# First layer of a two-layer graph network: x loads ahead of the adjacency, three quarters of the mask as strips on GpSimd

## The reference, cut to what matters

```
h = relu(layernorm(x))
q, k, v = h @ W.T + b, in 4 heads of 64
scores = clip(q @ k.T / 8, -10, 10), and -10 where adj == 0
attn = softmax(scores) within each chunk of 256 keys
out = (sum over the 8 chunks of attn @ v) @ Wo.T + bo + h
x = x + layernorm(out) * gamma + beta
...                         # second layer: softmax over neighbours of leaky_relu(ei + ej)
```

## Time and profile before

| | |
|---|---|
| median of 3 runs | 4966.05 us (4965.57 to 4966.41) |
| profiled execution | 4965.84 us, span 4964.0 us |
| busy, share of the span | TensorE 4617.1 us (93%), VectorE 3681.5 (74%), ScalarE 2924.1 (59%), GpSimd 1947.7 (39%) |
| mean of one clip (L512), of one exponential (L421) | 1216 ns, 1056 ns |
| mean granted TensorE clock | 0.98 |
| TensorE busy in 25 to 50, 50 to 75, 75 to 100, 107 to 175 us | 13.00, 25.00, 9.56, 67.60 us |
| GpSimd busy in 0 to 25, 50 to 150 us | 15.76, 0.00 us |

### The profile page before, as it was taken

The page is one execution under the profiler, slowest core; times in us unless marked ns, Lnnn a source line. Parts: engine busy times, 40 slices in busy tenths (PEclk is TensorE's granted clock), DMA queues, the critical chain, the costliest instruction groups (busy, mean ns, idle before and its releaser), DMA issues. The chain is left out here.

```text
span 4964.0 us, 78134 instructions
## 1 busy us (share of the span) xinstructions
PE 4617.1 (93%) x31752; PEld 2705.9 (55%) x31752; DVE 3681.5 (74%) x5434; ACT 2924.1 (59%) x3373; POOL 1947.7 (39%) x1391
## 2 busy tenths in 40 slices
PE   5999999998999999999999899947999999999998
PEld 2334333333433433433333343327999999999998
DVE  4676677678577677667767857747889889898896
ACT  3553555455455355355445545518878888788785
POOL 1133222232232223223223323225657576666585
PEclk9999999999999999999999999968999999999999
DMA  5000000000100000000000000011112112111111
GB/s 186 1 18 9 26 9 18 26 9 9 34 9 9 19 16 18 9 26 14 13 26 9 13 14 9 9 35 49 50 47 77 30 68 76 34 65 54 47 56 44
DMA packets 126665, 160.50 MB, mean 32 GB/s; under 512 B 8545, under 2 KB 108897, under 8 KB 126305
## 3 DMA queue, kind: packets, MB, share of 16 engines
q1 hardware_dynamic: 126304, 155.49, 9.7%
HBM read 121.64 MB, written 33.83 MB: 31 GB/s over the span
## 5 line engine op out<-in xcount | busy, mean ns | idle before, releaser
L421 ACT ACTIVATE e_sb<-e_sb 128x1024 f32<-128x1024 f32 x1024 | 1080.4, 1056 | 1186.6 <-DVE e_sb L512 1171.4
L512 DVE SCALAR_TENSOR_TENSOR e_sb<-psS,mask 128x1024 f32<-128x1024 f32 x1024 | 1225.8, 1216 | 473.8 <-PE psS L628 460.1
L1229 PE MATMUL psA<-xy,ring_p 128*128 128x195 bf16 x8192 | 1399.4, 248 | 19.6 <-DVE red L1109 19.6
L1229 PE MATMUL psA<-xy,ring_s 128*128 128x195 bf16 x8192 | 1399.0, 248 | 0.0
L628 PE MATMUL psS<-qT,kT 64*128 64x512 f32 x4096 | 1089.7, 617 | 57.3 <-DVE e_sb L512 57.3
L1029 ACT ACTIVATE ring_s<-eiB,ejb 128x1024 int8<-128x1024 f32 x1024 | 1088.5, 1135 | 8.5 <-PE psA L1229 8.5
L641 PE MATMUL psN<-e_sb,v_sb 128*64 128x512 f32 x4096 | 1000.1, 609 | 0.0
L352 POOL TENSOR_TENSOR ctxT<-ctxT,num 128x512 f32<-128x512 f32 x384 | 486.3, 1275 | 1009.0 <-DVE num L492 1009.0
L1229 PEld LDWEIGHTS psA<-xy,ring_p 128*128 128x128 fp8e4 x8192 | 799.5, 98 | 24.9 <-DVE red L1109 22.5
L1229 PEld LDWEIGHTS psA<-xy,ring_s 128*128 128x128 fp8e4 x8192 | 798.7, 97 | 8.0 <-issue 0.3
L628 PEld LDWEIGHTS psS<-qT,kT 64*128 64x128 f32 x4096 | 460.2, 187 | 464.2 <-issue 234.7
(11 more groups left out here) (104 smaller groups left out, 4010.5 us busy)
## 6 DMA issues: line engine op xcount, KB each, us to landing
eiB<-ei_between SPq DMA_DIRECT2D x64, 512.0 KB, 4.2
xin<-x SPq DMA_DIRECT2D x32, 512.0 KB, 6.7
xr<-x SPq DMA_DIRECT2D x32, 512.0 KB, 3.8
x_between<-hy SPq DMA_DIRECT2D x32, 512.0 KB, 2.9
xin<-x_between SPq DMA_DIRECT2D x32, 512.0 KB, 5.6
xo<-x_between SPq DMA_DIRECT2D x32, 512.0 KB, 4.4
out<-o_sb SPq DMA_DIRECT2D x32, 512.0 KB, 5.2
e_sb<-adjT SPq DMA_DIRECT2D x4, 2048.0 KB, 9.6
```

The lines of the kernel that those rows point to most:

```text
L421: act.activation(e_sb[:, s % ES], e_sb[:, s % ES], ACT.Exp, scale=SCALE).then_inc(exp_done, 1)
L512: dve.scalar_tensor_tensor(out=e_sb[:, s % ES], in0=psS[:, s % 2], scalar=-CLIP_RAW, in1=mask[:, kb, cols][:, None, :].to_broadcast([P, 2, ...
L1229: ins = pe.matmul(psA[:, i % BANKS, br * PARTS * XW:(br + 1) * PARTS * XW], part[:, n % RING, k, tt * TW + j * P:tt * TW + (j + 1) * P], x ...
```

## The change

x tiles 2 and 3 are issued ahead of any adjacency. Only the adjacency of query tile 0 is still loaded in two halves and converted by VectorE and ScalarE, now at v = 15 (`MASK_AT`), and the steps begin when these two are done. The adjacency of query tiles 1 to 3 comes as 24 strips of 2 key blocks x 512 columns (0.5 MB), which lie by turns in xr and hy, two buffers that the first layer uses later for the residual. Each strip is issued when the one before the last has been converted. GpSimd converts all of them, after its constants and ahead of its first sum. VectorE waits for eight strips at the first step of each further tile of the first batch; the first load of a residual waits for all 24. The next batch's x is issued behind the last strip.

```diff
-MASK_AT = 5
+MASK_AT = 15
...
+        strip = [v.rearrange("p j f -> p (j f)").bitcast(I32).rearrange("p (k w) -> p k w", k=2) for v in (xr[:, :, :], hy[:, :, :])]
+        STRIPS = BLK // 2
+
+        def strip_at(m):
+
+            t, k = m // STRIPS + 1, m % STRIPS * 2
+            return slice(k, k + 2), slice(t * TW, (t + 1) * TW)
+
...
+            def load_strip(m):
+                if m >= 2:
+                    sp.wait_ge(strip_done, m - 1)
+                blocks, cols = strip_at(m)
+                sp.dma_start(strip[m % 2], adj_v[:, blocks, cols]).then_inc(strip_in[m % 2], 16)
...
             def load_residual(b, t):
+                if b == 0 and t == 0:
+                    sp.wait_ge(strip_done, (T - 1) * STRIPS)
                 sp.wait_ge(x1_out, b * (16 * T) + 16 * t + 16)
...
-            load_adjacency(0)
             load_x(0, 2)
             load_x(0, 3)
-            load_adjacency(1)
-            load_adjacency(2)
-            load_adjacency(3)
+            load_adjacency()
+            for m in range((T - 1) * STRIPS):
+                load_strip(m)
...
             pool.wait_ge(const_in, 16 * NCONST)
+            for m in range((T - 1) * STRIPS):
+                blocks, cols = strip_at(m)
+                pool.wait_ge(strip_in[m % 2], 16 * (m // 2 + 1))
+                pool.tensor_scalar(mask[:, blocks, cols], strip[m % 2], 2 * CLIP_RAW, -CLIP_RAW, ALU.mult, ALU.add)\
+                    .then_inc(strip_done, 1)
...
-            act.wait_ge(mask_done[0], T)
-            act.wait_ge(mask_done[1], T)
+            act.wait_ge(mask_done[0], 1)
+            act.wait_ge(mask_done[1], 1)
...
+                    if b == 0 and s % STEPS == 0 and s:
+                        dve.wait_ge(strip_done, s // STEPS * STRIPS)
                     dve.wait_ge(scores_done, b * BSTEPS + s + 1)
...
-            dve.wait_ge(mask_done[0], T)
-            dve.wait_ge(mask_done[1], T)
+            dve.wait_ge(mask_done[0], 1)
+            dve.wait_ge(mask_done[1], 1)
```

More of the change, by code:

```diff
@@ L157, in layer0 @@
         mask_done = [sem(f"mask_done{i}") for i in range(2)]
+        strip_in = [sem(f"strip_in{i}") for i in range(2)]
+        strip_done = sem("strip_done")
         ident_done = sem("ident_done")
@@ L246, in load_x, with load_adjacency @@
                 sp.dma_start(xin[:, t], tile_of(x_v, b, t)).then_inc(x_in[t], 16)
-            def load_adjacency(t):
+            def load_adjacency():
                 for k in range(2):
-                    if t >= 1:
-                        sp.wait_ge(mask_done[k], t)
-                    sp.dma_start(stage[k], adj_v[:, 8 * k:8 * k + 8, t * TW:(t + 1) * TW]).then_inc(adj_in[k], 16)
+                    sp.dma_start(stage[k], adj_v[:, 8 * k:8 * k + 8, 0:TW]).then_inc(adj_in[k], 16)
+            def load_strip(m):
[3 more added lines that the diff above has]
+                sp.dma_start(strip[m % 2], adj_v[:, blocks, cols]).then_inc(strip_in[m % 2], 16)
             def load_residual(b, t):
+                if b == 0 and t == 0:
+                    sp.wait_ge(strip_done, (T - 1) * STRIPS)
                 sp.wait_ge(x1_out, b * (16 * T) + 16 * t + 16)
@@ L435, in _ @@
                 prepare(0, v)
[L436 to L439, removed]
+                if v == MASK_AT:
+                    act.wait_ge(adj_in[1], 16)
+                    act.activation(mask[:, 8:16, 0:TW], stage[1], ACT.Copy,
                                    bias=-CLIP_RAW, scale=2 * CLIP_RAW).then_inc(mask_done[1], 1)
-            act.wait_ge(mask_done[0], T)
-            act.wait_ge(mask_done[1], T)
+            act.wait_ge(mask_done[0], 1)
+            act.wait_ge(mask_done[1], 1)
             for b in range(nb):
@@ L549, in _ @@
                 prepare(0, v)
[L550 to L553, removed]
+                if v == MASK_AT:
+                    dve.wait_ge(adj_in[0], 16)
+                    dve.tensor_scalar(mask[:, 0:8, 0:TW], stage[0], 2 * CLIP_RAW, -CLIP_RAW,
                                       ALU.mult, ALU.add).then_inc(mask_done[0], 1)
             dve.wait_ge(consts_done, 1)
-            dve.wait_ge(mask_done[0], T)
-            dve.wait_ge(mask_done[1], T)
+            dve.wait_ge(mask_done[0], 1)
+            dve.wait_ge(mask_done[1], 1)
             for b in range(nb):
```

## The result

The changed kernel takes 4937.47 us (median of 6 runs, 4936.16 to 4939.30), the kernel before on the same chip 4966.23. The ratio is 0.9943 with a 95% interval of 0.993 to 0.9956: 28.8 us less. The forecast was 4938.9. The profiled execution of the changed kernel was the slowest of its six, 4939.30 us with a span of 4937.4; against the profiled 4965.84 it is 26.5 us less, where the sum said 26.9.

A forecast was written before the change was run, and what follows sets the result against it. TensorE, busy 93% of the span, was taken as the bound, with time to win only in its start-up waits. 10.7 + 16.5 - 0.3 = 26.9 us off 4965.84 gave 4938.9 us, range 4934 to 4945.

The forecast's parts named there:

- Step 1: Start-up loads: x tile 2 ahead of the adjacency lands at 15.1, first projection at 26.3; net gain 10.7 us.
- rival (a): Start-up loads: the queue mixes x with the adjacency, so x comes no earlier; only 16.5 us gained, 4949.3; 6%.
- The rule on shared ports: SBUF access: two-SBUF-input VectorE instructions and GpSimd instructions take turns, each for its whole length; forecast charged 0.2 us instead.
- Rival (c): Statistics chains and mask conversion: VectorE and GpSimd take turns, leaving 19.2 us of gain, 4946.6; 6%.
- Step 2: First projection to first scores: stays 45.6 us, no gain; slow first matmuls worth some 1.8 us either way.
- Step 3: First clip no longer waits for masks 2 to 4: gain 16.5 us, less 0.3 for VectorE's conversion meeting strips.
- Step 4: GpSimd's 24 strips: 1.3 us conversion, 3.8 us load, 2.6 us spacing, done at 91, at worst 106; cost nothing.
- the cover: Ahead of GpSimd's first sum at 134: 28 us to spare for strips; beyond it each microsecond would count in full.
- Sum: Whole kernel: 10.7 + 16.5 - 0.3 = 26.9 us gained at the head of the chain; nothing later changes.

The follow-up runs named there:

- e1: The kernel before with only the loads reordered, x tiles 2 and 3 ahead of the adjacency, all masks converted as before: 4954.71 us.
- e2: The changed kernel with its strips, but x tiles 2 and 3 loaded behind the adjacency of query tile 0 again: 4950.39 us.
- e8: The changed kernel with VectorE's half of the first mask converted four times, each behind a wait for the one before: 4948.24 us.
- e6: The changed kernel with 64 small identity matmuls on TensorE between the first transposes and the first projection: 4936.37 us.
- e9: e5 with ScalarE normalising x tile 3 behind the first k copies, plus 36 small identity matmuls ahead of TensorE's first transposes: 4923.66 us.
- e4: The changed kernel with each strip converted four times on GpSimd: 4937.93 us.
- e3: The changed kernel with each strip converted six times on GpSimd, one behind the other: 4994.64 us.
- e5: The changed kernel with the first batch's tile 0 copies into hT ahead of the statistics of tiles 2 and 3: 4928.46 us.

## Why the prediction was right

- **Step 1.** Landing of tile 2: 15.1 predicted, 15.17 measured. The rule used, that the queue finishes in order and a load lands behind the one before it by its own bytes, held to 0.1 us; rival (a) is out. The first projection: 26.3 predicted, 26.49 measured. `e1` prices the step alone at 10.8 us by its medians against 10.7 net, with the first projection 10.3 us earlier in its trace. The two chains beside GpSimd's constants took 4.35 and 4.37 us against 4.20 alone, 0.15 to 0.17 us each where I had 0.1.
- **The rule on shared ports.** I set SBUF — State Buffer, "SBUF: two separate sides", of the Trainium skill (it says this of GpSimd instructions that read SBUF) against 4.31 and 4.20 us and believed the rows. That was a misreading: the 0.11 us are its turns. In the old trace the two-input instruction at 11.48 took 0.25 us and the one at 12.94 took 0.20 where others take 0.16, and each ended within 0.02 us of a GpSimd select (0.24 us from 11.47 and from 12.88); the changed kernel has the same at 18.62, beside the cast at 18.56. GpSimd's instructions there are so short that most such waits don't show. With 1.05 us strips on the other side (`e2`) the traces show its turns exactly. The 2.28 us conversions (`e8`), which have one SBUF input and to which the part that I had quoted doesn't speak, take turns too. My number for the changed kernel stood, but for a reason that I had not given, that the strips start after the chains. Rival (c) deserved the condition "if strips and statistics overlap".
- **Step 2.** The projections took 73.51 - 26.49 = 47.0 us against 45.6. The 1.4 us are the k matmuls of tile 0, 6.61 against 5.17, inside the 1.8 kept for them. `e6` and `e9` show that idle time makes them slow. Why they took longer behind 13.3 us without work than behind 23.9 no run shows.
- **Step 3.** Scores of step 4: 79.7 predicted (90.1 less 10.7 and plus 0.3), 80.12 measured. The late first matmuls cost 1.4 us, and part came back. VectorE's chain of q, mask and v was to end 0.9 us behind the scores of step 0, so that their delay counted only beyond that; and the collision, for which I had charged VectorE 0.3, fell on GpSimd. That was luck: the conversion happened to begin 0.9 us ahead of the strip, and behind a strip just begun it would have lost 0.73 (`e8`). The first clip came at 74.79, 0.8 us outside my 73 to 74, now waiting 0.47 us for those scores. The granted clock stayed at 1.00 as said. The clips beside strips took 1219 ns, against 1213 and 1214.
- **Step 4.** Conversion: 1.3 taken, 1.04 measured, the lower bound. Load: 3.8 us taken, 4.8 measured, the mis-sized term: I had used a row with one load in flight, and here there are two. In `e4`, where the next load is issued only when the one before has landed, the median is 3.8 again. What delays them isn't shown: the two don't fill the queue, whose DMA share in half-microsecond windows of the changed kernel from 60 to 72 us falls to 0.14 between bursts. Spacing 2.9 in place of 2.6, the last strip over at 97.6 in place of 91 (106 at worst). It cost nothing, for the reason given, 37 us of waiting ahead of the first sum. What lies beyond the cover was right in size (`e3`: 57 us slower for a first sum 56 us late) and wrong at its edge (`e4`: 2.3 us late, nothing lost).
- **Sum.** 26.9 predicted, 26.5 between the profiled executions, 28.8 between the medians. The 2.2 us between these two are where the profiled executions lie: the changed kernel's 1.8 above its median, the other 0.4 below.

## What to carry to other kernels

A wait at the head of a serial kernel like this one is worth what the change takes off it, and where two such waits stand one behind the other they add up; look in the program order for what was queued ahead of the late thing, a load or a computation (`e5` won another 9 us by moving two copies of 0.6 and 0.7 us). Work moved onto an idle engine cost nothing here until the first thing that engine owes to the others, and a little beyond: work out its period, the time of that first debt and the break-even between them, with the load times of as many transfers in flight as there will be. And when that engine is GpSimd, look at what VectorE does in the same microseconds, since in the traces here they take turns.

## What the runs showed of the hardware

VectorE and GpSimd exclude each other for whole instructions in the two pairings below, whichever comes second waiting: a VectorE instruction of 0.16 us with two SBUF inputs took 0.89 to 0.95 us when it met a 1.05 us strip, and a 2.28 us conversion of int32 to int8 from SBUF and 1.04 us strips alternate (`e8`), at 3.01 us a conversion and up to 2.38 us a strip. The clip, with one input from PSUM and one from SBUF, is not touched (1219 ns beside strips, 1213 without).

The granted clock can read 1.00 while matmuls take twice their usual time. Here are 26 to 30 us of the changed kernel, by window as above:

```profile
26.00:30.00 4.00, 3.51 (x4) 1.51 (x5) 0.00 (x0) 0.39 (x1) 1.04 (x1) 1.00 0.64 237
```

In this window the first k matmuls run, of which the slowest took 1191 ns where later ones take 593, behind 13.3 us without work; with small matmuls in that gap the eight take 3.60 us (`e6`), as later ones do. So for the first real work on TensorE the duration of the matmul has to be read, and not the clock column alone.
